# A quantised feed-forward: bias inside the product, GELU read from PSUM, tiles one by one

## The reference

```
x  = x + tanh(g_ffn[1]) * ffn(layernorm(x))
ffn(h): h = gelu(bitlinear(h, w1, b1)); return bitlinear(h, w2, b2)      # 512 -> 2048 -> 512
bitlinear(x, w, b): einsum('bsd,hd->bsh', act_quant(x), weight_quant(w)) + b
act_quant(x):    scale = 127 / max(max|x| of the row, 1e-5)
                 clip(round(x * scale), -128, 127) / scale
weight_quant(w): scale = 1 / max(mean|w|, 1e-5)
                 clip(round(w * scale), -1, 1) / scale
```

## Time and profile before

| | |
|---|---|
| median of 3 runs | 2841.33 us (2840.94 to 2842.41) |
| the profiled execution | 2844.89 us |
| its span, first to last instruction | 2843.1 us |
| busy share of the span | PE 84%, DVE 62%, ACT 52%, POOL 38% |
| mean granted TensorE clock | 0.938 of full speed |
| last update of `x` before the feed-forward starts | 2647.96 us |
| first `norm` of the feed-forward starts (L2767) | 2703.72 us |
| last addition to `x` starts (L2799) | 2838.94 us |

### The profile page before, as it was taken

How to read it: one execution, slowest core, us unless ns; L and a number is a source line. 1 busy time by engine, 2 the same in 40 slices (tenths; PEclk the granted TensorE clock), 3 DMA queues, 4 the chain that set the end, 5 groups by cost and what they waited for, 6 DMA issues and landing times. The chain is left out here.

```text
span 2843.1 us, 46195 instructions
## 1 busy us (share of the span) xinstructions
PE 2385.3 (84%) x14782; PEld 1985.4 (70%) x14790; DVE 1755.0 (62%) x3889; ACT 1482.6 (52%) x3037; POOL 1086.3 (38%) x1545
## 2 busy tenths in 40 slices
PE   5999999999984888998887557999994798898355
PEld 3778788787874788888886446999983576677222
DVE  2555555555544666666664744556655787788486
ACT  3444444444433666666665454444432777778543
POOL 0322222322221444444442366777751644445000
PEclk9999999999996999999998777999997899999688
DMA  3000000000001000000001475677656422321100
GB/s 112 19 12 18 7 18 11 7 18 11 7 1 41 20 19 18 0 18 18 18 18 33 153 251 177 187 198 198 186 127 184 103 69 61 92 78 67 78 8 22
DMA packets 123652, 190.90 MB, mean 67 GB/s; under 512 B 18272, under 2 KB 66656, under 8 KB 121760
## 3 DMA queue, kind: packets, MB, share of 16 engines
q1 hardware_dynamic: 111408, 161.69, 18.9%
q0 software_dynamic: 10992, 25.96, 4.2%
q10 hardware_dynamic: 1152, 2.10, 0.3%
HBM read 143.58 MB, written 46.14 MB: 67 GB/s over the span
## 5 line engine op out<-in xcount | busy, mean ns | idle before, releaser
L435 ACT ACTIVATE x_p<-x_p,x_least 128x1024 f32<-128x1024 f32 x128 | 147.3, 1151 | 307.4 <-DVE x_least L391 307.4
L375 DVE TENSOR_TENSOR x_pT<-pair,x_pT 128x512 fp32r<-128x512 f32 x256 | 164.3, 683 | 122.4 <-ACT x_pT L454 122.4
L469 POOL TENSOR_TENSOR x_carry<-x_rtotal 128x1 f32<-128x1 f32 x128 | 24.7, 193 | 559.9 <-DVE x_rtotal L368 559.9
L2157 PE MATMUL pair<-m_h,e_w 128*128 128x320 f32 x1536 | 230.4, 310 | 1.1 <-DVE m_h L2072 1.1
L2157 PEld LDWEIGHTS pair<-m_h,e_w 128*128 128x128 f32 x1536 | 228.9, 189 | 2.7 <-issue 1.5
L537 PE MATMUL pair<-x_pT,x_v 128*128 128x256 f32 x1536 | 209.6, 293 | 9.2 <-DVE x_pT L375 9.2
L537 PEld LDWEIGHTS pair<-x_pT,x_v 128*128 128x128 f32 x1536 | 193.9, 194 | 26.3 <-issue 18.3
L993 ACT ACTIVATE s_p<-s_p,s_least 128x128 f32<-128x128 f32 (+3 forms) x256 | 143.6, 561 | 123.2 <-DVE s_least L903 123.2
L565 PE MATMUL pair<-x_kT,x_qT 128*128 128x512 f32 x768 | 207.0, 404 | 0.0
L2500 DVE TENSOR_REDUCE z_most<-pair 128x1 f32<-128x1008 f32 x128 | 154.0, 1203 | 72.8 <-PE pair L2610 50.9
L1131 PE MATMUL pair<-s_pT,s_v 128*128 128x256 f32 (+1 forms) x1152 | 158.5, 284 | 47.1 <-DVE s_pT L880 47.1
(11 more groups left out here) (337 smaller groups left out, 6108.5 us busy)
## 6 DMA issues: line engine op xcount, KB each, us to landing
e_raw<-in_L_ffn_w SPq DMA_DIRECT2D x48, 1024.0 KB, 5.8
z_v<-z_vst SPq DMA_DIRECT2D x16, 768.0 KB, 3.6
z_kS<-z_k SPq DMA_DIRECT2D x24, 512.0 KB, 10.3
z_vS<-z_v SPq DMA_DIRECT2D x8, 1536.0 KB, 6.5
f_raw<-in_L_ffn_w SPq DMA_DIRECT2D x2, 4096.0 KB, 13.4
z_qS<-z_q SPq DMA_DIRECT2D x24, 256.0 KB, 4.6
s_wraw<-in_L_ffn_wq SPq DMA_DIRECT2D x9, 512.0 KB, 4.4
x_wq<-in_L_xattn_Wq SPq DMA_DIRECT2D x8, 512.0 KB, 3.7
```

What stands on the lines that cost most here:

```text
L375: dve.tensor_tensor(pT[1][:, keys, q * P:(q + 1) * P], TR[j][:, :].rearrange("p (k n) -> p k n", n=P), pT[0][:, keys, q * P:(q + 1) * P].b ...
L435: act.activation(p[n][:, :], p[n][:, :], ACT.Exp, scale=-1.0, bias=least[:, n:n + 1], accum_out=total[:, n:n + 1]).then_inc(s_ex, 1)
L2157: mm = pe.matmul(GU[m % 2][:, j * BANK:j * BANK + CAP], w[x0][:, c, m * P:(m + 1) * P], XS[s][x1][:, c, :], start=(n == 0 and c == 0), sto ...
```

## The change

The tiles run one by one, in an order written out in full for each engine, three tiles ahead (`AHEAD = 3`), with semaphores of their own for each kind of step. `b1` goes into the hidden product: for each tile VectorE makes two columns from the tile's scale (a rounded part and the rest), twice, in `u` [128, 4]. TensorE turns `u` to `uT` [4, 128], and a product of `uT` with the four rows of `brows` (twice the rounded part of `b1`, twice the rest) opens each bank. GELU reads two banks at a time straight from PSUM and multiplies by the tile's scale. The clip of activations is left out. `b1` is loaded to 2 partitions instead of 128; ScalarE writes its rounded part, VectorE the rest, and a third, small transfer puts the rest on partitions 2 and 3 of `brows`. The diff, cut to its core:

```
-            b1, b2 = sb("f_b1", [P, HID]), sb("f_b2", [P, D])
+            brows, b2 = sb("f_brows", [4, HID], F32R), sb("f_b2", [P, D])
+            u = [sb(f"f_u{s}", [P, 4], F32R) for s in range(2)]
+            uT = [sb(f"f_uT{s}", [4, P], F32R) for s in range(2)]
...
-                sp.dma_start(b1[:, :], a["L1_ffn_b1"].partition_broadcast(P)).then_inc(s_b, 16)
+                sp.dma_start(braw[:, :], a["L1_ffn_b1"].partition_broadcast(2)).then_inc(s_b, 16)
                 sp.dma_start(b2[:, :], a["L1_ffn_b2"].partition_broadcast(P)).then_inc(s_b, 16)
+                sp.wait_ge(s_mean, 4)
+                sp.dma_start(brows[2:4, :].bitcast(F32), blow[:, :].bitcast(F32)).then_inc(s_b, 16)
...
# VectorE
+                dve.wait_ge(s_size, 4)
+                dve.tensor_tensor(blow[:, :], braw[:, :], brows[0:2, :].bitcast(F32), ALU.subtract).then_inc(s_mean, 1)
                 for g in range(1, 2 * GROUPS, 2):
...
-                    dve.tensor_scalar(src, src, MAGIC + TOP, MAGIC + BOTTOM, ALU.min, ALU.max).then_inc(s_r, 1)
...
-                def hidden(pair, s):
-                    for k in range(HB):
-                        dve.wait_ge(s_m1, 2 * HB * pair + HB * s + k + 1)
-                        cols = slice(k * BANK, (k + 1) * BANK)
-                        dve.scalar_tensor_tensor(z[s][:, cols], HID_B[k][:, :], unscale[:, s:s + 1], b1[:, cols],
-                                                 ALU.mult, ALU.add).then_inc(s_z, 1)
...
+                def norm(t):
...
+                    q = scales(h[s][:, :], t, 0)
+                    twice = q.to_broadcast([P, 2])
+                    step(dve.tensor_scalar(u[s][:, 0:4:2], twice, winv[:, 0:1], None, ALU.mult))
+                    step(dve.scalar_tensor_tensor(u[s][:, 1:4:2], twice, winv[:, 0:1], u[s][:, 0:4:2].bitcast(F32), ALU.mult, ALU.subtract))
+                    dve.tensor_scalar(h[s][:, :], h[s][:, :], q, MAGIC, ALU.mult, ALU.add).then_inc(s_rh, 1)
...
+                dve.wait_ge(s_b, 48)
+                for t in range(AHEAD):
+                    norm(t)
+                for t in range(NT):
+                    hidden_scale(t)
+                    if t + AHEAD < NT:
+                        norm(t + AHEAD)
+                    if t:
+                        add_out(t - 1)
+                add_out(NT - 1)
# ScalarE
+                    if w == 0:
+                        act.wait_ge(s_b, 32)
+                        act.activation(brows[0:2, :], braw[:, :], ACT.Copy).then_inc(s_size, 1)
...
+                    act.activation(uT[s][:, :], TRU, ACT.Copy).then_inc(s_eh, 1)
+                    act.activation(hqT[s][:, :, :], TRH[:, 0:KC * P].rearrange("p (c n) -> p c n", c=KC), ACT.Copy).then_inc(s_eh, 1)
...
+                    for j in range(2):
+                        act.wait_ge(s_m1, 2 * t + j + 1)
+                        act.activation(z[s][:, j * 2 * BANK:(j + 1) * 2 * BANK], HID2[j][:, :], ACT.Gelu,
+                                       scale=unscale[:, t:t + 1]).then_inc(s_g, 1)
...
+                norm_round(0)
+                norm_turned(0)
+                norm_round(1)
+                norm_turned(1)
+                gelu(0)
+                norm_round(2)
+                for t in range(NT):
+                    hidden_round(t)
+                    if t + 1 < NT:
+                        gelu(t + 1)
+                    if t + 2 < NT:
+                        norm_turned(t + 2)
+                    hidden_turned(t)
+                    if t + AHEAD < NT:
+                        norm_round(t + AHEAD)
# TensorE
+                    pe.wait_ge(s_eh, 2 * (t + 1))
+                    for k in range(HB):
+                        if t and k % 2 == 0:
+                            pe.wait_ge(s_g, 2 * (t - 1) + k // 2 + 1)
+                        cols = slice(k * BANK, (k + 1) * BANK)
+                        pe.matmul(HID_B[k][:, :], uT[s][:, :], brows[:, cols], start=True, stop=False)
                         for c in range(KC):
+                            mm = pe.matmul(HID_B[k][:, :], hqT[s][:, c, :], w1T[:, c, cols], start=False, stop=(c == KC - 1))
...
+                pe.wait_ge(s_b, 48)
+                norm_turn(0)
+                hidden(0)
+                norm_turn(1)
+                hidden(1)
+                norm_turn(2)
+                for t in range(NT):
+                    hidden_turn(t)
+                    if t + 2 < NT:
+                        hidden(t + 2)
+                    output(t)
+                    if t + AHEAD < NT:
+                        norm_turn(t + AHEAD)
```

More of the change, by code:

```diff
@@ L2658, in bit_ffn @@
             hqT = [sb(f"f_hqT{s}", [P, KC, P], BF16) for s in range(2)]
+            u = [sb(f"f_u{s}", [P, 4], F32R) for s in range(2)]
+            uT = [sb(f"f_uT{s}", [4, P], F32R) for s in range(2)]
+            with ExitStack() as early:
+                braw = early.enter_context(nc.sbuf_tensor("f_braw", [2, HID], F32))
+                blow = early.enter_context(nc.sbuf_tensor("f_blow", [2, HID], F32R))
             z = [sb(f"f_z{s}", [P, HID]) for s in range(2)]
@@ L2662, in bit_ffn @@
             o = [sb(f"f_o{s}", [P, D]) for s in range(2)]
[L2663 to L2667, removed]
+            most, scale = sb("f_most", [P, 2 * NT]), sb("f_scale", [P, 2 * NT])
+            unscale = sb("f_unscale", [P, 2 * NT])
+            HID_B, HID2, OUT_B = banks[0:HB], pairs[0:2], banks[4]
+            TRH, TRU = banks[5][:, :].bitcast(BF16), banks[5][0:4, 2 * P:3 * P]
+            TRZ = [banks[6 + i][:, :].bitcast(BF16) for i in range(2)]
             WTB = [pairs[2 + i // 2][:, (i % 2) * BANK:(i % 2 + 1) * BANK].bitcast(BF16) for i in range(4)]
             s_w = [sem("f_w1"), sem("f_w2")]
[L2671 to L2695, removed]
+            s_b, s_size, s_sum, s_mean, s_wr, s_wq, s_wt, s_wa, s_wd = [
+                sem(f"f_{n}") for n in ("b", "size", "sum", "mean", "wr", "wq", "wt", "wa", "wd")]
+            s_ch, s_rh, s_rz, s_qh, s_qz, s_th, s_tz, s_eh, s_ez, s_m1, s_g, s_m2, s_x2 = [
+                sem(f"f_{n}") for n in ("ch", "rh", "rz", "qh", "qz", "th", "tz", "eh", "ez", "m1", "g", "m2", "x2")]
+            CH, AHEAD = 4, 3
             def chunk(t3, k):
@@ L2745, in step, with scales @@
                     ins.then_inc(s_ch, 1)
-                    dve.wait_ge(s_ch, steps if i is None else first("steps", i) + steps)
-                def quantise(src, n, w, i):
+                    dve.wait_ge(s_ch, steps)
+                def scales(src, n, w):
                     m, q = most[:, n:n + 1], scale[:, n:n + 1]
[L2751 to L2755, removed]
-                    dve.tensor_scalar(src, src, MAGIC + TOP, MAGIC + BOTTOM, ALU.min, ALU.max).then_inc(s_r, 1)
@@ L2758, in tile @@
[L2758 to L2769, removed]
@@ L2781, in vector @@
[L2781 to L2801, removed]
@@ L2835, in scalar @@
                     turned(act, g)
[L2837 to L2842, removed]
-                    act.activation(dst, TRB[bank][:, 0:m * P].rearrange("p (m n) -> p m n", m=m), ACT.Copy).then_inc(s_te, 1)
-                def norm(rounded, turns):
-                    for s in range(2):
-                        whole(hq[s], h[s], rounded + s)
-                    for s in range(2):
-                        copy(hqT[s][:, :, :], turns + s, s, KC)
@@ L2851, in gelu @@
-                def gelu(pair):
-                    for s in range(2):
-                        act.wait_ge(s_z, HB * (2 * pair + s + 2))
-                        act.activation(z[s][:, :], z[s][:, :], ACT.Gelu).then_inc(s_g, 1)
-                norm(0, 0)
-                gelu(0)
-                norm(NORMED["rounded"], NORMED["turns"])
-                def body(i):
-                    rounded, turns = first("rounded", i), first("turns", i)
-                    for s in range(2):
-                        whole(zq[s], z[s], rounded + s)
-                        for k in range(2):
-                            copy(zqT[s][:, k * 8:(k + 1) * 8, :], turns + 2 * s + k, k, 8)
-                    if ahead(i, 1):
-                        gelu(i + 1)
-                    if ahead(i, 2):
-                        norm(rounded + HIDDEN["rounded"], turns + HIDDEN["turns"])
@@ L2894, in tensor @@
                 pe.wait_ge(s_wd, GROUPS)
-                def turn(src, n, bank, m):
-                    pe.wait_ge(s_te, n + 1)
-                    for k in range(m):
-                        mm = pe.transpose(TRB[bank][:, k * P:(k + 1) * P], src[:, k * P:(k + 1) * P], identb[:, :])
-                    mm.then_inc(s_tr, 1)
-                def norm(rounded, turns):
-                    for s in range(2):
-                        pe.wait_ge(s_q, rounded + s + 1)
-                        turn(hq[s][:, :], turns + s, s, KC)
@@ L2907, in hidden, with norm_turn @@
-                def hidden(pair, s, turns):
-                    pe.wait_ge(s_te, turns + s + 3)
+                def norm_turn(t):
+                    s = t % 2
```

(18 more changed lines are left out.)

122 lines of the change are left out of this document (73 added, 49 removed).

## The result

The changed kernel has a median of 2814.44 us over four executions (2811.63 to 2814.98), the kernel before 2841.87 beside it; the ratio of the means is 0.9898 (95% interval 0.9881 to 0.9915). It is faster by 27 us, about 1%; 2803.6 was forecast, and the upper end of the range was 2812. The profiled execution took 2814.98, with a span of 2813.2: 29.9 less than the profiled one of before.

What follows compares the result with a forecast made beforehand. VectorE's work plus stalls in the pairwise order was taken as the bound, TensorE after the change. Start, periods, drain, clock and four-row products sum to 98.3 against 135.97 us, so 2841.33 - 37.7 = 2803.6; range 2798 to 2812.

Steps and rivals of the forecast that it cites:

- The step that failed: TensorE, four-row bias products between full ones: 32 visits cost 0 to 6.4 us, 1.1 taken in the tiles' sum.
- Rival A: TensorE: every four-row visit costs the upper 0.2, or the product runs at half rate; 5.3 to 5.8 more, 2809; 14%.
- Its other form: TensorE: the four-row product runs at half rate, 32 x 0.216 = 6.9 us; within the 14% of Rival A.
- The range: Whole kernel, 8 in 10: median from 2798 to 2812 us, around a forecast of 2803.6.
- 2807.2: Whole kernel: forecast time of the profiled execution, which took 2844.89 before the change.
- periods exceed 10 us: Sign of being wrong: periods from reduction to reduction above 10 us, where 9.3 was forecast.
- moves by over 1 us: Sign of being wrong: the first `norm` moves by over 1 us, where still 2703.7 was forecast.
- Start, periods, drain: Tiles: start 17.0, first period 8.5, second 10.2, then 37.2 and 9.2, drain 13.4, slower clock at the end 1.7.
- Rival B: VectorE becomes the bound: with two small steps at 0.745 it has 10.0 per tile, 0.7 over TensorE; 2808.5; 8%.
- Costs taken as hidden: Ahead of the tiles: `b1` rounding 1.91 and VectorE's subtraction 2.29 fit in idleness; dropped broadcast gains 0 to 5.9, 0 taken.
- Table load: ScalarE, ahead of the first GELU: 1.28, hidden before and now exposed; by the skill page the sum is 1.4 longer.
- Rival D: TensorE stays at low clock, 1.2 instead of 2.4 GHz: a tile takes 18.0 us, 65 more in all, 2869; 3%.

## Why the prediction was wrong

The direction and the mechanism were right, a term of the sum was mis-sized; the median lies 2.4 us above the range.

- **The step that failed: "So a visit to few rows costs between nothing and 0.2 us: 32 visits, 0 to 6.4 us. I take 1.1", and with it "a load of weights is normally hidden under a 512-column product here".** The loads into and out of a four-row visit are not hidden: 0.31 between hidden products, 1.15 a tile in a steady period, so about 9 us over eight tiles (an estimate), beyond the upper end of 6.4. With 128 rows the tiles are 5.7 shorter (98.22 against 103.90), so that much came through. The forecast of 98.3 is met there partly by luck: without its 1.1 it is 97.2, and the second period was 1.8 over it, the start and the drain 0.5 each under it. My upper end was read from rows 7, where the products are short and the load stretches of 0.57 and 1.01 stand nearly end to end; what an open load costs in a stream of 512-column products can't be read there.
- **Rival A** (the visits dear) was the right case, but its price came from the same rows: 2809. Its other form, a product at half rate, is not what happened: with 128 rows five products take 1.11.
- **The range** took the earlier stages as fixed. They were 2.15 later in the profile of after (2705.87 against 2703.72), which with the 5.6 in the tiles makes the 7.8 by which the profiled execution (2814.98) missed 2807.2. The remaining 3 us of the miss of the median come from moving a difference between two profiles to medians: the profile before lay 3.56 above its median, the one after 0.54. So that the median fell outside the range is in part chance. The measured 32.1 in the tiles, taken off the 2841.33 of before, gives 2809.3, inside it; and eleven later executions of the kernel before have a median of 2845.15. The signs were clearer: "periods exceed 10 us" (10.25) and a first `norm` that "moves by over 1 us" (2.15) both came, the second from the earlier stages.
- **Start, periods, drain.** Forecast 17.0, first period 8.5, second 10.2, 46.4 for the other five, 13.4 + 1.7; measured 18.05, 9.01, 11.23, 51.26, 14.35; with 128 rows 16.47, 8.42, 11.96, 46.74, 14.63. The second period is furthest off there, by 1.8, and its granted clock is 0.86, where I had TensorE at full clock; with 96 rows it had 1.00 and took 10.29. In the changed kernel the first period had 0.66 and the second 1.00.
- **VectorE.** 8.9 per tile forecast, 8.80 to 8.84 as the floor without the bias product. The steps on `u` cancelled the clip of `norm`. Rival B didn't happen.
- **Costs taken as hidden.** The rounding of `b1` (1.89) delayed no last chunk: that one still had its 0.55 of idleness. VectorE's subtraction (2.27) fitted ahead of its third copy, which then still waited 1.52. Between the first chunk on VectorE and the first `norm` lie 2705.87 - 2674.18 = 31.69 us, against 31.77 before. The 1 MB less to load brought nothing: ScalarE waited 5.92 for the second matrix, 5.9 before.
- **Table load.** 1.28 again, exposed as forecast. The Trainium skill (ScalarE: Activation LUTs, What ACT_TABLE_LOAD costs) gives 1283 ns for the load itself and adds about 1380 ns of drain for every switch. The first is what the trace has, the second doesn't show: in the changed kernel the load starts 0.02 after the copy ahead of it, and GELU 0.02 after the load. The measurement decides.

```profile
2719.88 0.57 ACT L2822 ACTIVATE f_hqT<-pair 128x512 bf16<-128x512 bf16 x1
2720.47 1.28 ACT L2828 ACT_TABLE_LOAD   x1
2721.77 2.12 ACT L2828 ACTIVATE f_z<-pair,f_unscale 128x1024 f32<-128x1024 f32 x2
```

- **Rival D** (low clock): not seen in the steady part, where the granted clock is 1.00. It shows ahead of the second reduction (0.79 in the start, 0.66 in the first period) and in the drain: the last 16 products took 4.11 in the changed kernel's first profile and 5.72 in its second, which is 1.6 and covers the 1.4 between tiles of 103.90 and 105.30. The forecast had 3.45 + 1.7.

```profile
2804.08 4.11 PE L2924 MATMUL pair<-f_w2T,f_zqT 128*128 128x512 bf16 x16 [0.35 <-ACT f_zqT L2844]
```
```profile
2803.19 5.72 PE L2924 MATMUL pair<-f_w2T,f_zqT 128*128 128x512 bf16 x16 [0.35 <-ACT f_zqT L2844]
```

## What to carry to other kernels

A product of few rows put between full ones for its small size is not small: it has its columns' time and, here with 4 and with 64 rows, two weight loads that stand open, its own and that of the product behind it, instead of running beside a product. Padding its operands with zero rows makes it cost little more than its columns (1.11 for five products, 1.08 in bfloat16), and gathering such products pays the price once for the group. When a term has no row, take the bound from a row whose neighbours are as long as those of the new place, and count how often it occurs before giving it a small value.

## What the hardware showed that I had not expected

- The price of a four-row product between 512-column ones: 0.28 us with float32r operands, 0.21 in bfloat16 (banks of 1.39 and 1.29 against 1.11 and 1.08 with 128 rows). It is close to the sum of the two weight loads in and out. In float32r it is the same with 64 rows and gone with 96.
- The earlier stages, the same code in every run, end up to 10 us apart from profile to profile, and eleven executions of the kernel before span 16 us; the tiles' steady periods are the same to 0.01 us (10.25 and 10.26 in both profiles of the changed kernel).
